# Attention scores as extra columns of the first weight pieces, and the work that moves with them

## What is computed

```python
def rgcn(x, W, root, b):            # three layers; relation r = 0..3
    return x @ root + b + sum(A[r] @ (x @ W[r]) for r in range(4))   # A[r]: edge counts / degree
def gcn(x, W, b):                   # two layers
    return A_sym @ (x @ W) + b
def gat(x, W, a_src, a_dst, b, heads):        # four layers: 4, 1, 8, 1 heads
    h = (x @ W).reshape(n, heads, c)
    al_s = einsum('nhc,hc->nh', h, a_src)     # one number per node and head
    al_d = einsum('nhc,hc->nh', h, a_dst)
    e = leaky_relu(al_s[src] + al_d[dst], 0.2)
    alpha = softmax of e over the edges that enter one dst
    return segment_sum(h[src] * alpha, dst) + b
```

## Time and profile before

| what | value |
| --- | --- |
| median of 3 runs | 1563.07 us (1562.09 to 1565.7) |
| the profiled execution, its own time | 1569.24 us |
| span in its profile | 1567.5 us |
| granted TensorE clock, mean | 0.951 |
| PE busy | 1448.0 us, 92% |
| DVE busy | 795.4 us, 51% |
| POOL busy | 541.2 us, 35% |
| weight load of 192 KB, issue to landing | 2.4 us |

### The profile page before, as it was taken

How to read it: one execution, slowest core, us unless ns; L and a number is a source line. 1 busy time by engine, 2 the same in 40 slices (tenths; PEclk the granted TensorE clock), 3 DMA queues, 4 the chain that set the end, 5 groups by cost and what they waited for, 6 DMA issues and landing times.

```text
span 1567.5 us, 22867 instructions
## 1 busy us (share of the span) xinstructions
PE 1448.0 (92%) x7912; PEld 1325.1 (85%) x7912; DVE 795.4 (51%) x1887; ACT 417.2 (27%) x871; POOL 541.2 (35%) x607
## 2 busy tenths in 40 slices
PE   5899789999999999999999999899888998897896
PEld 3567689999999999999999989798777976786873
DVE  7978645233544365562324345462564124499443
ACT  1163511111110111110101221444562434445431
POOL 5210342334243443353343223252444534223330
PEclk9998899999999999999999999899999998967899
DMA  3100111112334242341121211221012101100001
GB/s 113 46 19 13 36 46 41 41 51 62 95 100 133 61 114 78 102 133 50 50 61 50 61 31 41 62 79 39 26 46 83 52 21 49 57 1 1 11 1 49
DMA packets 57653, 86.49 MB, mean 55 GB/s; under 512 B 6442, under 2 KB 54183, under 8 KB 57433
## 3 DMA queue, kind: packets, MB, share of 16 engines
q1 hardware_dynamic: 45184, 66.02, 14.4%
q10 hardware_dynamic: 12374, 19.17, 4.1%
HBM read 83.24 MB, written 1.92 MB: 54 GB/s over the span
## 4 chain that ended last, share of the span: by engine, by line
PE 72%; DVE 17%; ACT 4%; issue 3%; POOL 2%; DMA 1%; ACTq 0%; DVEq 0%; SPq 0%; POOLq 0%
PE psum L2209 13%; PE psum L2212 13%; PE psum L2213 13%; PE psum L2226 7%; PE psum L2229 7%; PE psum L2660 4%; DVE max_scratch L1940 2%; PE psum L2314 2%; PE psum L2694 2%; POOL w_lo L822 1%; DVE onehot_dst L1490 1%; PE psum L2270 1%; PE psum L2550 1%; PE psum L2554 1%; PE psum L2555 1%
## 5 line engine op out<-in xcount | busy, mean ns | idle before, releaser
L2209 PE MATMUL psum<-w_lo,xT_hi 128*125 128x384 f32 (+2 forms) x1200 | 413.4, 344 | 10.8 <-POOL w_lo L822 3.8
L2212 PE MATMUL psum<-w_hi,xT_lo 128*125 128x384 f32 (+2 forms) x1200 | 406.8, 339 | 0.0
L2213 PE MATMUL psum<-w_hi,xT_hi 128*125 128x384 f32 (+2 forms) x1200 | 405.9, 338 | 0.0
L809 POOL CAST w_hi<-w_raw 128x384 fp32r<-128x384 f32 x190 | 103.6, 545 | 504.7 <-PE psum L2213 495.2
L2209 PEld LDWEIGHTS psum<-w_lo,xT_hi 128*125 128x125 f32 (+1 forms) x1200 | 225.9, 188 | 15.8 <-POOL w_lo L822 6.1
L1526 DVE TENSOR_TENSOR h_lo<-psum,h_hi 125x384 fp32r<-125x384 f32 (+1 forms) x120 | 66.9, 557 | 316.2 <-ACT h_hi L990 315.2
L2212 PEld LDWEIGHTS psum<-w_hi,xT_lo 128*125 128x125 f32 (+1 forms) x1200 | 226.2, 189 | 0.2
L2213 PEld LDWEIGHTS psum<-w_hi,xT_hi 128*125 128x125 f32 (+1 forms) x1200 | 225.7, 188 | 0.0
L811 POOL TENSOR_TENSOR w_lo<-w_raw,w_hi 128x384 fp32r<-128x384 f32 x190 | 200.8, 1057 | 15.2
L2226 PE MATMUL psum<-h_lo,adjacency 125*125 125x384 f32 (+3 forms) x600 | 204.0, 340 | 1.7 <-ACT adjacency L1030 1.7
L990 ACT ACTIVATE h_hi<-psum 125x384 fp32r<-125x384 f32 (+1 forms) x120 | 59.1, 492 | 545.6 <-PE psum L2213 536.7
(11 more groups left out here) (313 smaller groups left out, 2152.1 us busy)
## 6 DMA issues: line engine op xcount, KB each, us to landing
w_raw<-weights_dram SPq DMA_DIRECT2D x296, 192.0 KB, 2.4
score_w_raw<-weights_dram ACTq DMA_DIRECT2D x58, 192.0 KB, 2.9
x_nat<-x_dram SPq DMA_DIRECT2D x1, 1875.0 KB
x_residual<-x_dram SPq DMA_DIRECT2D x1, 1875.0 KB
out_dram<-x_residual SPq DMA_DIRECT2D x5, 375.0 KB
score_a_rows<-L_gnn_a_src_dram ACTq DMA_DIRECT2D x8, 192.0 KB, 3.4
score_a_rows<-L_gnn_a_dst_dram ACTq DMA_DIRECT2D x8, 192.0 KB, 4.9
rgcn_bias<-rgcn_bias_dram SPq DMA_DIRECT2D x1, 1125.0 KB
```

The lines of the kernel that those rows point to most:

```text
L809: nc.gpsimd.tensor_copy(mem.wh[:, slot, :], mem.raw[:, raw_slot, :]).then_inc(w_hi_ready, 1)
L2209: ins = nc.tensor.matmul(o, h, wl, start=(j == 0), stop=False, skip_group_check=True)
L2212: nc.tensor.matmul(o, l, wh, start=False, stop=False, skip_group_check=True)
L2213: ins = nc.tensor.matmul(o, h, wh, start=False, stop=stop and j == k - 1, skip_group_check=True)
```

## The change

**Scores as columns.** The ring slots of `w_hi` and `w_lo` get a pitch of 400 columns instead of 384, the weights in 0 to 383 and score weights behind them. DVE's `scores_split` writes the split score weights there, into the slots of the layer's first piece, where it wrote `wa_hi` and `wa_lo`. `first_piece` multiplies 384 + 2·heads columns (392, 386, 400, 386), and waits for the score weights before its first block. `early_scores` and its 156 matmuls (36, 48, 36, 36) are gone. ACT copies each block's score columns from PSUM to `al`, ahead of the feature copy of that block (five small copies).

**Rows turned from columns as two parts.** DVE splits the source scores (`al_parts`, two small instructions between its wait for `al` and L1921). PE turns them, five transposes to 2·heads rows, one chunk step into `chunks_and_scores` instead of ahead of it. ACT copies the result to `al_T`, now fp32r, in two instructions. `send_row` multiplies it with `row_select`, which sums the two parts, with fp32r operands for the 512 columns and f32 for the 113. The first row of each layer is sent at step 2 instead of 1, `turn_columns` and `send_columns` of Q1 to Q3 at 4 and 5 instead of 3 and 4, and Q2's second row after the last chunk step instead of at step 5.

**Remainders of the first 20 chunks by DVE.** `weights_lo` on DVE writes them: 0 to 4 before the sorting, 5 to 9 behind it, 10 to 14 after tile 8 of sweep 2, chunk 15 after tile 32 of it, 16 to 19 after the last tile of sweep 3. POOL begins with chunk 20.

**RGCN layer 0, first half.** `over` for columns 0 to 511 of a relation stood before the aggregation of the unit before, and now stands behind it; `over` for the remaining columns follows at the beginning of the next relation.

**Per-tile waits.** In Q1 and Q3 the first `sum_tile` waits for each source tile by itself instead of all five. Addresses of small buffers move.

```diff
-               {1: (0,)}, {3: ("turn", 0), 4: ("send", 0)}, {0: ((3, (0,), 0), (6, (), NB))})
+               {2: (0,)}, {4: ("turn", 0), 5: ("send", 0)}, {0: ((3, (0,), 0), (6, (), NB))})
...
-               {1: (0,), 5: (1,)}, {3: ("turn", 0), 4: ("send", 0)}, {0: ((3, (0,), 0), (4, (), NB))})
+               {2: (0,)}, {4: ("turn", 0), 5: ("send", 0)}, {0: ((3, (0,), 0), (4, (), NB))})
...
+        WEIGHTS_AFTER = {(2, 8): (WRING, 15), (2, 32): (15, 16), (3, GROUP - 1): (16, 2 * WRING)}
...
-            out.append(("sorted",))
+            out += [("weights", 0, RAW), ("sorted",), ("weights", RAW, WRING)]
...
-            split_lo(0, 2 * WRING)
+            pool.wait_ge(w_lo_ready, 2 * WRING)
...
+                    if g < NB:
+                        ins = nc.scalar.activation(mem.al[0:BP, m, 0:2 * q.heads], bank(bank_, HW, HW + 2 * q.heads), ACT.Copy)
+                        if g == NB - 1:
+                            ins.then_inc(al_ready, 1)
...
+            def weights_lo(a, e):
+
+                for c in range(a, e):
+                    dve.wait_ge(w_hi_ready, c + 1)
+                    nc.vector.tensor_tensor(mem.wl[:, c % WRING, :], mem.raw[:, c % RAW, :],
+                                            mem.wh[:, c % WRING, :].bitcast(F32), ALU.subtract).then_inc(w_lo_ready, 1)
...
+                link(nc.vector.tensor_copy(hi_, mem.al[0:BP, :, 0:q.heads]))
+                nc.vector.tensor_tensor(lo_, mem.al[0:BP, :, 0:q.heads], hi_.bitcast(F32), ALU.subtract).then_inc(al_split, 1)
...
-                    if l == 0 and f == 0 and i % NB == NB - 1:
-                        pe.wait_ge(counts_lo_ready, (i // NB + 1) * NB)
-                        over(2 * (i // NB), counts_of(i // NB), 0, 512)
+                    if l == 0 and i % NB == 0 and i + f:
+                        r = (f * H_UNITS + i) // NB - 1
+                        if r < NREL:
+                            over(2 * r + 1, counts_of(r), 512, NC)
...
             def turn_scores(q):
 
-                pe.wait_ge(al_copied, 2 * (q.index + 1))
+                pe.wait_ge(al_split, q.index + 1)
+                if not q.residual:
+                    pe.wait_ge(gemm_read, q.gemm0 + NB)
...
-                    ins = nc.tensor.transpose(bank(7, m * 16, m * 16 + w), mem.al_T[0:w, nodes(m)], mem.ident[0:w, 0:w])
+                    a = row_col(q) + (m * BP if m < NB - 1 else 512)
+                    ins = nc.tensor.transpose(ps[0:w, a:a + BP], mem.al_parts[0:BP, m * w:(m + 1) * w].bitcast(F32),
+                                              mem.ident[0:BP, 0:BP])
...
+                    one, row = mem.row_sel[0:w, h:h + 1], mem.al_T[0:w, a:z]
+                    if (z - a) % 2:
+                        one, row = one.bitcast(F32), row.bitcast(F32)
+                    ins = nc.tensor.matmul(ps[0:BP, p:e], one.to_broadcast([w, BP]), row, start=True, stop=True)
```

More of the change, by code:

```diff
@@ L511, in adjacency_plan @@
                     out.append(("tile", s, t))
+                    if (s, t) in WEIGHTS_AFTER:
+                        out.append(("weights",) + WEIGHTS_AFTER[s, t])
                     if t in ROOTS_AFTER[s]:
@@ L1513, in _ @@
                     dve.wait_ge(consts_ready, 4)
+                elif step[0] == "weights":
+                    weights_lo(*step[1:])
                 elif step[0] == "lower":
@@ L1746, in scores_split @@
             def scores_split(i):
-                w = LAYERS[i].k * 2 * LAYERS[i].heads
-                s = mem.sums[i][:, :, :, :].rearrange("p k s h -> p (k s h)")
-                link(nc.vector.tensor_copy(mem.wa_hi[:, 0:w], s))
-                nc.vector.tensor_tensor(mem.wa_lo[:, 0:w], s, mem.wa_hi[:, 0:w].bitcast(F32), ALU.subtract
-                                        ).then_inc(wa_ready, 1)
+                q = LAYERS[i]
+                w, first = 2 * q.heads, q.chunk % WRING
+                s = mem.sums[i][:, :, :, :].rearrange("p k s h -> p k (s h)")
+                n = min(q.k, WRING - first)
+                for a, slot, e in ((0, first, n), (n, 0, q.k)):
+                    if a < e:
+                        hi_, lo_ = (t[:, slot:slot + e - a, HW:HW + w] for t in (mem.wh_pads, mem.wl_pads))
+                        link(nc.vector.tensor_copy(hi_, s[:, a:e, :]))
+                        ins = nc.vector.tensor_tensor(lo_, s[:, a:e, :], hi_.bitcast(F32), ALU.subtract)
+                        if e < q.k:
+                            link(ins)
+                ins.then_inc(wa_ready, 1)
             def beside(l, f, i):
@@ L2546, in chunk_step @@
                         pe.wait_ge(gemm_read, q.free_count(g))
-                    if j == 0 and piece == 1 and q.banks[g] == 7 and not q.residual:
-                        pe.wait_ge(al_ready, q.index + 1)
                     o, h, l = bank(q.banks[g], 0, width), xh[:, j, nodes(m)], xl[:, j, nodes(m)]
@@ L2724, in chunks_and_scores @@
                 for step in range((len(q.pieces) - 1) * q.k):
+                    if step == 1:
+                        turn_scores(q)
                     for h in q.rows_at.get(step, ()):
```

105 lines of the change are left out of this document (42 added, 63 removed).

## The result

| | kernel before | changed kernel |
| --- | --- | --- |
| median, first runs | 1562.58 us (1559.64 to 1565.7) | 1551.01 us (1550.1 to 1555.68) |
| ratio | | 0.9927 (0.9913 to 0.9941) |
| profiled execution, its time | 1569.24 us | 1551.1 us |
| PE busy | 1448.0 us | 1408.1 us |

The account below looks back on a forecast made before the run. PE, busy 92%, was taken as the bound, with DVE limiting some stretches. Q0 −8, Q1 −13.5, Q2 −4.7, Q3 −4.9, early phase −3.5, `over` −0.5, wider pieces +1.1 gave −34: 1535 profiled, 1529 from the median; range 1518 to 1543.

Parts of the forecast that it names:

- first rival: POOL and weights cap Q1 at −8, the counting gives nothing: −22 us in all, or 1541; chance 0.2.
- All of it lies on PE's path.: Q1's 48 early-score matmuls, 6.86 us with no waits between; with Q0, Q2 and Q3, 22.2 us go.
- The terms for rows and chain: Q0: chain of four rows, maxima and scores behind them shortens by about 3 us, four rows × 0.8.
- fourth rival: Sent rows with fp32r cost what f32 rows cost: +5 us, 1534; inside the 0.62 case.
- five terms: Q1: early scores −6.9, ACT's copy −1.95, low clock −1.6, row numbers −2.7, row −0.8; together −14 us.
- lock rival: POOL's long instructions lock out DVE's small score splits: 1 to 1.5 us per layer, +5, 1534; inside the 0.62 case.
- the 0.8 us that I counted for the per-tile waits: Q3's sums: PE works during the 3.0 us wait for all tiles, giving 0.8 us back.
- six rows on the path: Of 14 rows sent, eight lie in DVE-limited Q2, so six count, at 0.8 us saved each.
- Q2's terms: Q2: early scores −5.1, later rows +1.0, loop over heads −0.5; sum given as −4.7 us, bounds −2 and −6.
- Early phase: Counting, first 20 remainders moved to DVE: −1.9 + 3.2 − 4.1, with the fill −3.5 us; bounds −7 and +3.
- Wider pieces: First pieces of Q0 to Q3: 2580 added columns cost 1.1 to 1.2 us; bounds 0 and 3.
- rival on the pitch: Products reading 400-column slots each cost over 7.7 ns more, making the kernel slower; 1573 at 10 ns; chance 0.03.

Follow-up runs that it names:

- e1: Kernel before with the early scores cut from 156 products to 8, nothing else changed: ratio 0.9962 to the kernel before.
- e4: Changed kernel with ACT's copies of the last block ahead of its casts of the last three weight chunks: ratio 0.9881 to the kernel before.
- e8: Kernel before with early scores cut to 8 products and ACT's last-block copies ahead of its casts of the last chunks: ratio 0.9894 to the kernel before.
- e5: Changed kernel with POOL's five residual sums of 768 columns in Q1 cut to 8 columns: ratio 0.9877 to the kernel before.

## Why the prediction was wrong

**The sign and the list of edits were right, the sum was not.** The forecast was −34 us (range −20 to −45), the time was −11.5. Half of my first rival came true: Q1 gives next to nothing, for POOL and the weight stream, but I gave it 0.2 and let it keep 8 us of gain in Q1.

**The step that failed: "All of it lies on PE's path."** I read in the earlier trace rows that no product waited in or behind the early scores, and concluded that their removal moves all that follows. In Q2 and Q3 this held (4.2 and 4.6 us of 5.1 in e1), in Q0 and Q1 not at all (0 of 5.1, 0 of 6.9). The rows that speak against it were in the trace: in both layers ACT's last casts begin when PE begins its last block (1010.96 in Q0, above, and 1191.37 in Q1, after ACT had stood 6.54 us), the copy stands behind them, and in Q1 the last of them waited 1.71 us for a load. I had seen that one, behind the 1.95 us in the earlier trace rows, and counted its wait as gone, since "the transposes now stand behind a step of 15 products". But the copy still stood behind the same casts, and its next waiter was the chunk step itself, which needs the PSUM bank. e1, e4 and e8 show this: 4.5 and 6.3 us of new or longer waits for ACT with the scores cut and nothing else changed, and 5 and 8 us back in Q0 and Q1 with the copy moved.

**Q0, −8 forecast, −3.5 found.** The wait for ACT took 2.6 us of it, and the low clock behind it about 1.4: with the copies first (e4) Q0 is 7.6 us shorter than before, the number that I had forecast. The terms for rows and chain were right in size. A row now costs 0.62 us (0.5 forecast, 1.26 before):

```profile
1014.20 0.69 PE L2628 MATMUL psum<-al_rows,row_select 8*125 8x512 f32 x3
1014.82 0.44 PE L2579 MATMUL psum<-w_lo,xT_hi 128*125 128x384 f32 x1
```

This answers to the earlier trace rows, and the fourth rival falls.

**Q1, −13.5 forecast, −1.0 found.** Of the five terms, 6.9 became a wait of 4.33; the 1.95 and the low clock came back with it (granted clock 0.73 from 1186.60 to 1193.00 us, 0.72 before in the earlier trace rows); the 2.7 for the row numbers turned into +2.0, since I left DVE's chain as long as before, when its small instructions took 3.6 us beside the tail of POOL's sums, and gave the new meeting no price. The bound for Q1's loss was too narrow: I gave POOL's pace 0.5 us from one row pair, where the right question was what on DVE and ACT stands beside that series once PE is earlier.

**The lock rival.** I priced it on the split of the scores (1 to 1.5 us in each layer) and it was not there: in Q0, Q1 and Q2 the split took 0.4 to 1.2 us, in Q3 2.4, and PE waited for it by some 0.2 us at most (Q3, where the transposes start at 1480.85, just as the split ends). The lock's price was at the six small instructions behind the maxima, with 6.9 us in one layer. Section "🔬 SBUF: two separate sides" of the page "SBUF — State Buffer" in the Trainium skill says that whichever of the two starts first holds the shared ports for the whole instruction. The trace agrees: 0.17 us instructions took 0.9 to 1.8, the length of a POOL instruction of 1.0 or 1.8, and in e5, without the long ones, five of the six took 0.16 to 0.18.

**Q2 and Q3.** −3.8 and −3.4 of −4.2 and −4.9. In e1, which has neither the later step nor the per-tile waits, they are −4.2 and −4.6. At Q3's sums PE now waits 5.18 us for ACT's features, where it had waited 3.01 for DVE's tiles. ACT copies the features after the exponentials, so PE's first sum waits for these whatever the tiles' waits are, and the 0.8 us that I counted for the per-tile waits could not come. I had counted six rows on the path, but the sums hold only the five of Q0 and Q1; and Q2's terms give −4.6, not −4.7.

**Early phase, −3.5 forecast, −0.7 found.** The undisturbed one-hots came as forecast. The first one-hot came 1.0 us earlier (53.60 against 54.6) instead of 1.9, PE's wait in sweep 2 was 6.7 us (DVE's 7.9 us were right, with 7.7 from tile 8 to tile 9, but none of it overlapped with its earlier idleness), and the four remainders behind the last tile (1.96 us) were missing from my sum.

**Wider pieces.** Products of 392 columns start 0.18 us apart, as forecast:

```profile
995.82 0.34 PE L2235 MATMUL psum<-w_lo,xT_hi 128*125 128x392 f32 x1
996.00 0.34 PE L2238 MATMUL psum<-w_hi,xT_lo 128*125 128x392 f32 x1
```

Chunk products from slots of the new pitch keep their 0.175 us, so the rival on the pitch falls. **`over`** waits 3.7 instead of 6.7 us, as forecast; its worth at the end can't be told from zero.

## What to carry to other kernels

Work that PE does without waiting may still be what lets other queues catch up. Before counting it as a gain, list what each other engine does in that time and what stands in its queue ahead of the next thing that PE needs: here three casts that wait for loads stood ahead of a 0.7 us copy, and the removal gained 17 us with the copy moved, where it gained 6 alone. When a wait has been taken away, look where the same engine's work meets the rest next; POOL's 11 us of sums cost about the same at four places.

## What the runs showed that I had not expected

- A wait can cost more than its length. Behind the 2.60 us in Q0 the granted clock was 0.50 for 2.9 us, and taking the wait away gave 4 us. But the length of the wait alone does not tell the clock behind it: behind 2.54 us at Q3's sums it was 1.00 in one kernel and 0.74 in another.
- Small VectorE instructions are held one by one, not for a whole series of GpSimd's: in e4 they ended 5.4 us before the series did.
- Two long stretches scatter by several us between single profiles of one and the same code: 828.2 to 834.7 us from the counting to Q0 in the changed kernel, and 107.8 to 113.7 us in Q2's heads over the thirteen profiles whose code is equal there. A sum made against one profiled execution carries that. The one of the kernel before was 6 us above the median, and both stretches were on the high side in it, as far as its code can be compared with the others'.
